# Jump announcements in the band and head loops, and band projections two groups ahead, in a four-stage transformer block

## The reference, cut to what matters

```python
x = x + attn_a(layernorm(x))   # 16 heads of 8, a band: left context 25, chunks of 10
x = x + ffn(layernorm(x))      # 32 experts, top 8, and a shared one
x = x + attn_b(layernorm(x))   # 16 heads of 8, all keys, softmax over the heads
x = x + ffn(layernorm(x))
```

## Time and profile before

| | us |
|---|---|
| median of three runs | 2259.34 (2257.16 to 2259.64) |
| the profiled execution | 2251.4 |
| its span on the core | 2249.6 |
| band stage, first SP issue to last DVE addition | about 63 to 310 |
| head stage, steady part | about 740 to 1885 |
| PE busy over the span | 1965.4 (87%) |
| POOL busy over the span | 1476.5 (66%) |

### The profile page before, as it was taken

How to read it: one execution, slowest core, us unless ns; L and a number is a source line. 1 busy time by engine, 2 the same in 40 slices (tenths; PEclk the granted TensorE clock), 3 DMA queues, 4 the chain that set the end, 5 groups by cost and what they waited for, 6 DMA issues and landing times. The chain is left out here.

```text
span 2249.6 us, 59182 instructions
## 1 busy us (share of the span) xinstructions
PE 1965.4 (87%) x21978; PEld 1301.0 (58%) x21978; DVE 1735.0 (77%) x2431; ACT 1248.6 (56%) x2205; POOL 1476.5 (66%) x1044
## 2 busy tenths in 40 slices
PE   1688873999965999999999999999999997399997
PEld 1465562444433766777676777677777775244443
DVE  5465576666676988999898999889998897666665
ACT  2344442666643655666565666666666664266664
POOL 3100000656664988999898999889999995065564
PEclk9999976999986999999999999999999998599999
DMA  3221111995201000000000000000000000089731
GB/s 117 64 65 59 51 43 40 175 190 137 67 0 39 9 15 11 14 10 16 10 16 9 16 11 14 12 13 12 9 9 6 9 5 1 17 177 171 163 81 37
DMA packets 94204, 108.02 MB, mean 48 GB/s; under 512 B 31504, under 2 KB 55696, under 8 KB 93584
## 3 DMA queue, kind: packets, MB, share of 16 engines
q1 hardware_dynamic: 91136, 102.75, 19.7%
q10 hardware_dynamic: 2832, 1.79, 0.3%
HBM read 87.52 MB, written 16.99 MB: 46 GB/s over the span
## 5 line engine op out<-in xcount | busy, mean ns | idle before, releaser
L1172 POOL TENSOR_TENSOR ffn_exp_sw<-ffn_exp_sg,ffn_exp_wide 128x512 f32<-128x512 f32 x256 | 324.7, 1268 | 606.6 <-DMA ffn_exp_wide<-pair_weights 402.5
L958 DVE TENSOR_REDUCE head_shift<-head_score 128x64 bf16<-128x1024 f32 x512 | 625.6, 1222 | 125.2 <-PE head_score L770 112.5
L920 ACT ACTIVATE head_ex<-head_score 128x1024 f32<-128x1024 f32 x512 | 524.8, 1025 | 233.0 <-PE head_score L792 231.4
L727 POOL TENSOR_TENSOR head_half<-head_ex 128x1024 f32<-128x1024 f32 x256 | 605.0, 2363 | 28.7 <-ACT head_ex L920 28.7
L965 DVE TENSOR_TENSOR head_ex<-head_ex,head_recp 128x1536 f32<-128x1536 f32 x256 | 446.6, 1744 | 5.7 <-ACT head_recp L892 5.7
L802 PE MATMUL head_den<-head_half,c_ident 128*128 128x128 f32 x3072 | 392.9, 278 | 3.6 <-POOL head_half L728 2.9
L802 PEld LDWEIGHTS head_den<-head_half,c_ident 128*128 128x128 f32 x3072 | 370.5, 195 | 7.8 <-POOL head_half L728 3.4
L734 POOL TENSOR_TENSOR head_ex<-head_ex,head_recip 128x512 f32<-128x512 f32 x256 | 328.9, 1285 | 50.7 <-ACT head_recip L894 43.2
L792 PE MATMUL head_score<-head_shift,c_identb 128*128 128x512 bf16 x1024 | 312.1, 387 | 43.3 <-issue 25.8
L770 PE MATMUL head_score<-att_b_HB,att_b_GR 96*128 96x256 f16 x2048 | 314.0, 276 | 11.0 <-DMA att_b_HB<-b_queries 10.5
L1283 DVE TENSOR_TENSOR ffn_exp_h_parts<-ffn_exp_hidden,ffn_exp_h_parts 128x512 f16<-128x512 f32 x272 | 188.0, 691 | 174.5 <-ACT ffn_exp_h_parts L1243 173.4
(11 more groups left out here) (205 smaller groups left out, 2557.4 us busy)
## 6 DMA issues: line engine op xcount, KB each, us to landing
ffn_exp_wide<-pair_weights SPq DMA_DIRECT2D x256, 256.0 KB, 8.6
a_keys<-band_parts_k SPq DMA_DIRECT2D x13, 295.5 KB, 2.5
att_a_HB<-a_keys SPq DMA_DIRECT2D x52, 73.9 KB
a_queries<-band_parts_q SPq DMA_DIRECT2D x13, 271.5 KB, 2.9
att_a_GR<-a_queries SPq DMA_DIRECT2D x13, 271.5 KB
b_queries<-head_parts_q SPq DMA_DIRECT2D x32, 96.0 KB, 1.6
att_b_HB<-b_queries SPq DMA_DIRECT2D x128, 24.0 KB
b_keys<-head_parts_k SPq DMA_DIRECT2D x24, 96.0 KB, 1.6
```

The lines of the kernel that those rows point to most:

```text
L727: ch.link(pool.tensor_tensor(hf, e[:, 0:8, :], e[:, 8:16, :], ALU.add))
L920: act.activation(ex[:, kt % RING, :, h * QS:(h + 1) * QS], score[:, h, :, :].rearrange("p k (a w) -> p (k a) w", a=NH // 2), ACT.Exp, scal ...
L958: dve.tensor_reduce(shift[:, h, :], score[:, h, :, :].rearrange("p k (a w) -> p w k a", a=NH // 2), AX.XY, ALU.max, negate=True).then_inc( ...
L1172: pool.tensor_tensor(sw[:, g % 2, :], sg[:, g % 2, :], wide[:, g // NU, i, :], ALU.mult).then_inc(sw_ready, 1)
```

## The change

Two things change. First, the loops of the band stage and of the head stage are made with `hint_back_edge=True`: on each engine that runs such a loop, the first instruction of every iteration is a BRANCH_PREFETCH_HINT that names the jump at the loop's end and its target. A loop that runs only once gets none. Second, the band's projections run two groups ahead instead of one: the parts have two buffers, the queries of the group after the next are projected in the first tile of a group and its keys in the second, both into `bank_q`. The first two groups are projected before the loop, the second into the still unused banks `num` and `den`, and the first values into `turned`. SP places 14 groups instead of 13. Because the buffer must be a constant, ACT now loops twice over two batches, and DVE writes batches 0 and 1 out, and has a loop of one trip for 2 and 3.

```diff
-        parts_q, parts_k = m.sb("parts_q", [P, SLOTS, QCOLS], F16), m.sb("parts_k", [P, SLOTS, KCOLS], F16)
+        parts_q, parts_k = m.sb("parts_q", [P, 2, SLOTS, QCOLS], F16), m.sb("parts_k", [P, 2, SLOTS, KCOLS], F16)
...
-            return (b * NGRP + 1 + -(-t // GT)) * 2
+            return (b * NGRP + 2 + t // GT) * 2 + t % GT
...
-            for n in range(B * NGRP + 1):
+            for n in range(B * NGRP + 2):
                 place(n, n % NGRP)
...
-                    if t % GT == 1:
-                        pe.wait_ge(low_ready, ONE + units_before(b, t))
-                    values(b, (t + 1) * QT if t < NQT - 1 else S, tile + 1)
+                    values(b, (t + 1) * QT if t < NQT - 1 else S, tile + 1, bank_v)
...
-                    if t % GT == 0:
-                        ahead = (t // GT + 1) * GT * QT if t // GT < NGRP - 1 else S
+                    if t % GT < 2:
+                        group = t // GT + 2
+                        ahead = group // NGRP * S + group % NGRP * GT * QT
                         pe.wait_ge(added, ONE + outs_before(b, t + 1))
-                        project(b * S + (ahead + LEFT), QCOLS, bank_q, 0)
-                        pe.wait_ge(v_done, ONE + tile + 2)
-                        project(b * S + ahead, KCOLS, bank_v, 1)
...
+                        pe.wait_ge(low_ready, ONE + units_before(b, t))
+                        project(b * S + (ahead + (0 if t % GT else LEFT)), KCOLS if t % GT else QCOLS, bank_q, t % GT)
...
-            with pe.Fori(1, B) as b:
+            with nc.Fori(1, B, engines=[pe.engine], hint_back_edge=True) as b:
...
-            with act.Fori(0, B) as b:
-                batch(b)
...
+            with nc.Fori(0, B // 2, engines=[act.engine], hint_back_edge=True) as two:
+                batch(two * 2, 0)
+                batch(two * 2 + 1, 1)
...
-                    if t % GT == 1:
-                        low_parts(b * NGRP + (t // GT + 1))
+                    if t % GT > 0:
+                        low_part(b * NGRP + (t // GT + 2), (par + t // GT) % 2, t % GT - 1, bank_q)
...
-                with eng.Fori(0, (NQ - 2) // 2) as pair:
+                with nc.Fori(0, (NQ - 2) // 2, engines=[eng.engine], hint_back_edge=True) as pair:
...
-            with pool.Fori(1, B * NQ) as n:
+            with nc.Fori(1, B * NQ, engines=[pool.engine], hint_back_edge=True) as n:
```

More of the change, by code:

```diff
@@ L408, in project, with values @@
                 product(pe, bank[:, 0:cols], w, u, xh, xl).then_inc(qk_ready, 1)
-            def values(b, first, tile):
+            def values(b, first, tile, bank):
                 w = c["a_parts"]
@@ L416, in values @@
                     high, low = xnT[:, 0, at], xnT[:, 1, at]
-                    out = bank_v[0:KWIN, j * E:(j + 1) * E]
+                    out = bank[0:KWIN, j * E:(j + 1) * E]
                     pe.matmul(out, high, w[:, 2, 0, :], start=(j == 0), stop=False, skip_group_check=True)
@@ L520, in _, with high_part, batch @@
             m.start(act, "act")
-            def high_part(n, bank, parts, cols, u):
+            def high_part(n, buf, u, bank):
+                parts, cols = (parts_q[:, buf, 0:3:2, :], QCOLS) if u == 0 else (parts_k[:, buf, 0:2, :], KCOLS)
                 act.wait_ge(qk_ready, ONE + n * 2 + u + 1)
-                if u == 0:
-                    act.wait_ge(written, ONE + n * (WRITES * 16))
                 act.activation(parts, bank[:, 0:cols][:, None, :].broadcast_to([P, 2, cols]),
                                ACT.Identity, bias=c["a_bias"][:, u:u + 1]).then_inc(high_ready, 1)
[L529 to L533, removed]
+            def batch(b, par):
                 for t in range(NQT):
@@ L541, in batch @@
                         act.activation(probT[:, h, :], turned[:, h, :], ACT.Copy).then_inc(probT_ready, 1)
-                    if t % GT == 0:
-                        high_parts(b * NGRP + (t // GT + 1))
-            high_parts(0)
-            with act.Fori(0, B) as b:
-                batch(b)
+                    if t % GT < 2:
+                        n = b * NGRP + (t // GT + 2)
+                        if t % GT == 0:
+                            act.wait_ge(written, ONE + n * (WRITES * 16) - WRITES * 16)
+                        high_part(n, (par + t // GT) % 2, t % GT, bank_q)
+            for g, banks in enumerate(((bank_q, bank_v), (num, den))):
+                for u in range(2):
+                    high_part(g, g, u, banks[u])
+            with nc.Fori(0, B // 2, engines=[act.engine], hint_back_edge=True) as two:
+                batch(two * 2, 0)
+                batch(two * 2 + 1, 1)
         @block.vector
@@ L551, in _, with low_part, place_values @@
             m.start(dve, "dve")
[L553 to L559, removed]
+            def low_part(n, buf, u, bank):
+                parts, low, cols = (parts_q, 1, QCOLS) if u == 0 else (parts_k, 2, KCOLS)
+                dve.wait_ge(high_ready, ONE + n * 2 + u + 1)
+                dve.scalar_tensor_tensor(parts[:, buf, low, :], bank[:, 0:cols], c["a_bias"][:, u:u + 1], parts[:, buf, 0, :],
+                                         ALU.add, ALU.subtract).then_inc(low_ready, 1)
+            def place_values(tile, buf, bank):
                 dve.wait_ge(v_ready, ONE + tile + 1)
@@ L563, in place_values @@
                     slots = vw[e * KWIN:(e + 1) * KWIN, buf * NSUB * NG:(buf + 1) * NSUB * NG, :].rearrange("p s (r w) -> p s r w", w=16)
-                    heads = bank_v[0:KWIN, :].rearrange("p (s r w) -> p s r w", r=2, w=16)
+                    heads = bank[0:KWIN, :].rearrange("p (s r w) -> p s r w", r=2, w=16)
                     last = dve.tensor_scalar(slots[:, :, 0:3:2, e * D:(e + 1) * D], heads[:, :, :, e * D:(e + 1) * D],
@@ L584, in add_output, with batch @@
                 dve.tensor_tensor(xt, xt, bank_q[:, 0:E], ALU.add).then_inc(added, 1)
-            def batch(b, first):
+            def batch(b, par, first):
                 for t in range(NQT):
@@ L592, in batch @@
                                           AX.X, ALU.max, negate=True).then_inc(shift_ready, 1)
-                    if t % GT == 1:
-                        low_parts(b * NGRP + (t // GT + 1))
+                    if t % GT > 0:
+                        low_part(b * NGRP + (t // GT + 2), (par + t // GT) % 2, t % GT - 1, bank_q)
                     if not (first and t == 0):
                         divide(tile - 1, (t - 1) % NQT)
-                    place_values(tile + 1, (t + 1) % GT)
+                    place_values(tile + 1, (t + 1) % GT, bank_v)
                     if out_tile(t) is not None and not (first and t == 0):
@@ L601, in batch @@
                         add_output(b, t)
[L603 to L607, removed]
+            for g, banks in enumerate(((bank_q, bank_v), (num, den))):
+                for u in range(2):
+                    low_part(g, g, u, banks[u])
+            place_values(0, 0, turned[:, 0, :])
+            batch(0, 0, True)
+            batch(1, 1, False)
+            with nc.Fori(1, B // 2, engines=[dve.engine], hint_back_edge=True) as two:
+                batch(two * 2, 0, False)
+                batch(two * 2 + 1, 1, False)
             divide(B * NQT - 1, NQT - 1)
```

16 lines of the change are left out of this document (9 added, 7 removed).

## The result

| | before | after |
|---|---|---|
| median, us | 2259.49 (2257.16 to 2262.07, 4 runs) | 2232.07 (2225.30 to 2238.46, 4 runs) |
| ratio, 95% interval | | 0.9878 [0.9847, 0.9909] |
| the profiled execution, its span | 2251.4, 2249.6 | 2231.58, 2229.8 |

A forecast was written before the change was run, and what follows sets the result against it. PE and POOL were taken as nearly full in the head stage, PE's waits as setting the band's pace. Head 31 plus band 24 (9 + 13 + 4 - 2) made 55 us: 2204 us, range 2188 to 2236.

The forecast's parts named there:

- Announcements of POOL, ACT and DVE, "I take 0": Loops on these engines: announcements hidden behind other work on POOL, cost 0; 15 us if 0.5 us beyond cover, 30 times.
- The third rival: POOL's loop: announcing makes the sequencer refetch its target and wait, 82 us lost against 55 gained, 2286 us; chance 0.07.
- Head jumps, 31: Head stage: announcing shortens eight PE jumps; 35.4 us of POOL idle less 2.4 and 2; bounds 20 and 35.
- a second stop behind the target: Head stage: code behind a jump's target also comes late, up to 2.5 us for two jumps; 2 us allowed.
- with the size of the body: PE's loops: a jump's length goes with the loop's instruction count, not with what waits around it; 3.45 us median in head.
- The clock: Head stage: granted clock falls behind PE's stop, lengthening POOL's gap; 0.96 over that iteration, 0.99 over the stage.
- the whole memory: PE's head loops: by the skill's 2048 instructions they fit, so announcing gains nothing, sum 24 instead of 55; trace disagrees.
- Band jumps, 9: Band stage: two PE jumps fall from 8.2 us to 2 x 0.3, gain 7.6, plus 1.5 from the clock; bounds 6 and 13.
- The second stop: Band stage: PE's 3.1 us stop behind the jumps' target stays, and may grow by about as much as was hidden.
- Waits for a group, 13: Band stage: PE's eight waits, 11.0 us, all go, with some clock gain; the first, 6.3, stays; bounds 9 and 14.
- Bank_v, 4: Band stage: 8.5 us wait for the keys' low half goes, up to 7.4 comes back in the third tile; bounds 1 and 8.
- The stage's end, -2 (2.4): Band stage's end: SP waits for an unneeded extra group, landing 2.4 us past DVE's end; cost 2, bounds 0 and 4.

The follow-up runs named there:

- e8_pe_and_pool: The changed kernel with announcements on PE and POOL only, none on ACT and DVE; 2210.01 us, ratio 0.9801 to the kernel before.
- e1_pe_only: The changed kernel with announcements on PE alone; 2208.27 us, ratio 0.9793 to the kernel before.
- e4_pe_slot0: e1_pe_only with all five PE loops placed at the start of a 256-instruction block; 2188.71 us, ratio 0.9706 to the kernel before.
- e5_slot0_no_announcement: e4_pe_slot0 with the same loop places but no announcement on PE either; 2235.42 us, ratio 0.9908 to the kernel before.
- e2_no_announcement: The changed kernel with all announcements off, only the projections two groups ahead left; 2243.64 us, ratio 0.9948 to the kernel before.
- e7_slot0_12_groups: e4_pe_slot0 with SP placing only the 12 groups that are used; 2191.84 us, ratio 0.9713 to the kernel before.

## Why the prediction was wrong by half

**Announcements of POOL, ACT and DVE, "I take 0".** This is the step that failed: the term that was put at nothing. Its working looked at POOL alone, and asked what the instruction costs where it stands. POOL is as forecast (`e8_pe_and_pool`). ACT and DVE cost 19 to 24 us together (`e1_pe_only` against the changed kernel), most of the 27.6 us that are missing. The price isn't the announcement's 0.03 to 0.06 us and isn't at the jump: it is stops of 0.4 to 8.2 us later on, six of the eight in code that is written out behind an announced loop, two (DVE, 1316 and 1621 us) at the start of the next loop or in its first iteration. Without the announcement there is none. The third rival had the right family (announcing in a loop whose jump was short can make code that would have been at hand late), but on POOL and at each jump; it is wrong in both, and it was too unlikely at 0.07. Why an announced loop lets its engine stop later, and why POOL is spared, the runs don't show.

**Head jumps, 31.** With ACT, DVE and POOL silent the head stage gains 27.7 us, within the bounds of 20 and 35. The reason that I gave for the shortfall was another: I allowed 2 us for a second stop behind the target, read from POOL's longer gaps in batches 0 and 1. In the kernel before PE's rows have no such stop above 0.66 us; the jumps of batch 1 are themselves longer (4.4 and 4.5 us, the others 3.3 to 3.7), and the later gaps go down to 2.5 us, not to 3.7. The loss is at the jumps themselves, four of which stay 1.8 to 3.9 us long since the loops of batches 1 and 2 reach into a ninth block. With all eight short (`e4_pe_slot0`) the gain is 32.0, net of the 3.7 us that the entry into the first loop now takes. That a jump's length goes "with the size of the body" was half of it: unannounced, the same loops cost 3.3 to 3.9 us at both places tried (3.3 to 4.5 in the kernel before); announced, they cost 0.23 if they fit in eight blocks. The clock behaved as expected: over 813 to 890 us, nearly the window of the earlier trace rows, with one short jump in it, it is 1.00 where the earlier trace rows had 0.96.

```profile
813.00:890.00 77.00, 75.85 (x988) 57.21 (x987) 71.78 (x61) 51.00 (x94) 74.39 (x52) 1.00 0.04 10
```

The Trainium skill, "Runtime: NRT & Kernel Launch", section "Instruction fetch mechanics", gives PE's memory 2048 instructions. That is the eight blocks of 256 within which the jumps became short. `e5_slot0_no_announcement` shows what the figure leaves out: an iteration of 1,924 that starts a block is not at hand at its jump unless it was announced. Fitting in is necessary here and not sufficient. The section's sentence on branches speaks of a target that "isn't in the current 2-page window", not of the whole memory as my prediction took it. With the long unannounced jumps the trace agrees; but an announced jump back across eight blocks (`e4_pe_slot0`) took 0.23 us and no packet came on queue 8, so for that case the measurement decides against two pages.

**Band jumps, 9.** The jumps went from 5.2 and 4.4 us to 1.4 and 1.7, not to 0.3. With 2,554 instructions, ten or eleven blocks, none of the four places tried made both of them short. The second stop stayed, as forecast, and grew by 2.1 us to 5.2 in all. So PE's stops at the two jumps went from 11.3 to 7.1 us, a gain of 4.1 where the term had 9, and against `e2_no_announcement` the announcement of PE gained the band only 2.3 us (the next stage at 291.87 instead of 294.15). This is the second term that was mis-sized.

**Waits for a group, 13.** The mechanism was right: the eight waits are gone, and only the start's is left, now 7.0 us. What that gave in time was not measured by itself.

**Bank_v, 4.** The wait for the low half went, and 8.7 us before the output product came. Whether this is the low half in the third tile, as the bound supposed, was not tried. The whole of the projections' part, group waits and bank_v and the end, gave about 13.8 us in the band (16.7 less the 2.9 of shorter stops, `e2_no_announcement`) where 15 were forecast. Over the kernel it was 11.7, since the head stage lost time.

**The stage's end, -2 (2.4).** It measured 3.0 us (3.7 instead of 0.7), and `e7_slot0_12_groups` shows its cause, the places of groups that nobody needs.

Put together: 18.5 of the band's 24, 12.4 of the head's 31, and -9.9 in a stage that the sum didn't hold.

**The better version.** `e4_pe_slot0` beats both kernels, 0.9706 [0.9689, 0.9723] against 0.9878: announce on PE only, with the loops at the start of a block. `e7_slot0_12_groups` can't be told from it.

## What to carry to other kernels

Announce a jump only on the engine whose jump row is long; on an engine that jumps in 0.05 us there is nothing to gain, and the harm appears later, in code and in a stage that the diff doesn't touch, so look over the whole trace for "issue" stops that were not there. Where a loop is near the size that its engine can hold, its place counts too (20 us by the ratios here, beside 35 for the announcement on PE): shift its head and read the length of each taken jump apart, since a median of twelve hides that four are not short. And cost an edit that is made on four engines once for each of them.

## What the runs showed of the hardware

- An announced loop of up to eight blocks of 256 instructions jumped back in 0.22 to 0.25 us on PE and fetched nothing more (`e4_pe_slot0`, and batches 0 and 3 of the changed kernel); one that reached 15 to 19 instructions into a ninth block took 2.9 to 3.9 us, about what it took unannounced (3.3 to 3.9).
- In the band, with more blocks, announced jumps took 0.34 to 2.06 us, and not in the order of the instructions ahead of them. What else enters is open.
- A placed loop has its own small bill: at slot 0 1.76 us of stop on PE behind the band loop (`e4_pe_slot0`) and 3.3 to 3.7 us at the first head loop's entry, which took 0.3 at slots 140 and 224.
- ACT's stop of 8.2 us ended 0.8 us after an 8 KB packet of instructions that took 3.0 us, where the DMA engines were 92% busy with weights; DVE's of 2.7 us ended 1.4 us after a packet of 0.3 us, where nothing else moved.
